# The feed forward's layer norm with its tokens on partitions

## The chip, the cores and the metric

The kernel runs on one core of a Trainium2 chip, in one launch. The metric is device time in microseconds (us); lower is better. The kernel before was timed in three runs: 2013.35 us is their median, 2007.73 the lowest and 2013.68 the highest. One execution was also profiled.

## What is computed

The input is one sequence of 2048 tokens with 128 channels. First comes an RWKV time mix with its own output norm (it takes the first 200 us and is not touched). Then come six layers, each an attention and a feed forward, both with a residual, and at the end a layer norm. Cut to what matters:

```python
def ffn_layer(x, g, bln, W1, b1, W2, b2):
    mu = x.mean(-1, keepdims=True)
    var = ((x - mu) ** 2).mean(-1, keepdims=True)
    xn = (x - mu) / jnp.sqrt(var + 1e-05) * g + bln
    hg = xn @ W1 + b1
    a, gate = jnp.split(hg, 2, -1)
    return a * jax.nn.gelu(gate, approximate=False) @ W2 + b2

for i in range(DEPTH):                      # DEPTH = 6
    x = attn_layer(shift_tokens(x), Wqkv[i], q_scale[i], k_scale[i], Wo[i]) + x
    x = ffn_layer(shift_tokens(x), ln_g[i], ln_b[i], W1[i], b1[i], W2[i], b2[i]) + x
```

`attn_layer` projects to 16 heads of 64, norms q and k to unit length, rotates them and attends inside windows of 32 tokens. `shift_tokens` takes half of the channels from the token before. All of it is float32.

## The kernel before, in words

The residual stream lies in two buffers, `xa` and `xb`, with the 128 channels on partitions and the tokens along the free axis. The 16 tiles of 128 tokens in 6 layers give 96 tile steps, and these are pipelined in software. Step `s` of `layers` (the functions `step` at L1011, L1048, L1145 and L1257, one for each engine) works on several tiles at once: it projects, norms and rotates q and k of tile `s+1` (live "p"), turns q and k of tile `s`, scores it and takes its softmax (live "a"), and does the mix with v, the output projection and the residual of tile `s-1` (live "b"). The feed forward goes by pairs of tiles, 256 tokens at a time, so that a part of it is in every second step:

- an **odd step** has "norm", the statistics of one pair's layer norm, and "down", the second matrix of an earlier pair;
- an **even step** has "up", which scales the pair whose statistics were taken in the odd step before, and multiplies it by the first matrix.

Each engine executes its own instructions strictly in the order written in its `step`, and waits on semaphores. Nothing else sets the order: there is no planner. A waiting instruction so holds up everything written behind it on its engine. Two places matter here. On PE, the order at the end of a step is v projection (L1352), down (L1359), the norm's matmul (L1364), the spread of the scale (L1371), the output projection `w_o` (L1377), the variance (L1383), `widen` (L1264), and then the next step's transposes of the probabilities (L1247). The latter wait for DVE's residual add `xb` (L1223), because `w_o`'s result lies in the bank that they write. On DVE the order is `unit` (L1176, twice), the first `centre_scores` (L1165, L1168), `norm_n` (L1214), the second `centre_scores`, `xa` (L1219), `xb` (L1223), `var_f` (L1228), `along` of k (L1234).

The layer norm is taken with the channels on partitions, so that its sums run across partitions, and PE does them:

1. POOL lays the shifted pair out in `shift_f` (L1025, L1026).
2. PE multiplies it by `centre`, which is the identity minus 1/128 everywhere: the result in `bank_b` is x minus its mean (L1364).
3. ACT copies that to `dev` (L1128) and squares it to `dev_sq` (L1130).
4. PE multiplies each tile of `dev_sq` by a column of 1/128: a variance for each token, tokens on partitions (L1383).
5. DVE adds the epsilon, from PSUM to `var_f` (L1228), and POOL raises it to the power -1/2, `rstd_f` (L1040).
6. In the even step ACT scales the rows of the identity by it, `rstd_diag` (L1098, twice), and PE multiplies that by ones: every partition now has every token's scale, in `bank_s` (L1371).
7. DVE multiplies `dev` by it, `norm_n` (L1214), ACT applies g and b of the norm, `normed` (L1121), and PE multiplies by the first matrix (`widen`, L1264).

POOL meanwhile does the rotation of q and k, all SBUF to SBUF on 128x1024 elements: `across` (L999) of q, `along` (L1032) of q, `rotated` (L1006) of q, `across` of k, [the power, in odd steps,] `rotated` of k. The `along` of k is DVE's (L1234). The first `across` of a step waits for DVE's `unit` of q.

The last norm, after the layers (`last_norm`, L1401), is written the other way: it turns the stream to tokens on partitions and uses DVE's batch-norm statistics (L1441, L1444) and a two-column `tensor_scalar` (L1450). It is not touched.

## Time and profile before

| what | value |
|---|---|
| median of 3 runs | 2013.35 us |
| span of the profiled execution, first to last instruction | 2010.7 us |
| PE busy (matmul) | 1805.9 us, 90% |
| DVE busy | 1557.0 us, 77% |
| POOL busy | 1455.2 us, 72% |
| ACT busy | 1164.3 us, 58% |
| mean granted TensorE clock | 0.969 of full |

The profile gives no time of its own for the profiled execution besides its span; the median of the runs is 2.65 us longer than that span. A busy share says how long an engine had an instruction in flight. It says neither that the engine was the limit nor that it ran at its best: the order of the queues and the last wait of each step say that.

### The profile page before, as it was taken

To read this page: it belongs to the slowest core of one execution; us is meant where nothing else is said; L and a number is where in the kernel's file an instruction comes from. 1 tells how busy PE (TensorE), PEld (TensorE's weight loads), DVE (VectorE), ACT (ScalarE), POOL (GpSimd) and SP (SyncE) were. 2 spreads that over 40 slices of the span, in tenths; PEclk is the share of its full clock that TensorE was granted. 3 is DMA by queue.
4 is the path that set the end of the run, shared out by engine and by line. 5 is a ranking of instruction groups with operands and counts; after the bars stand their busy time and mean duration, and the time that the engine had idled before them with its cause. 6 is when DMAs were issued, how large, how long until landed. Compare 5 with 4: busy or idle time off the path is not lost. (4 is left out here: it accounts for less than half of the span.)

```text
span 2010.7 us, 85596 instructions
## 1 busy us (share of the span) xinstructions
PE 1805.9 (90%) x34280; PEld 1311.9 (65%) x34280; DVE 1557.0 (77%) x2776; ACT 1164.3 (58%) x1966; POOL 1455.2 (72%) x967
## 2 busy tenths in 40 slices
PE   7774689999999999999999999999999999999995
PEld 3453466676776666766666666667676667676764
DVE  4764688887888878888788788887887888878864
ACT  2311356666666666666666666666666666666662
POOL 3221688877887778777877787778777877787771
PEclk9875899999999999999999999999999999999997
DMA  4000122223222223222223322233222232222220
GB/s 151 2 3 1 44 65 65 59 54 86 73 70 53 55 63 91 59 70 63 61 53 84 77 68 55 52 82 81 63 58 59 63 86 63 70 63 55 55 58 22
DMA packets 93581, 123.43 MB, mean 61 GB/s; under 512 B 27760, under 2 KB 41808, under 8 KB 93392
## 3 DMA queue, kind: packets, MB, share of 16 engines
q1 hardware_dynamic: 93232, 122.42, 24.2%
q8 instruction: 46, 0.75, 0.2%
q10 hardware_dynamic: 288, 0.13, 0.0%
q14 instruction: 15, 0.12, 0.0%
HBM read 20.74 MB, written 1.05 MB: 11 GB/s over the span
## 5 line engine op out<-in xcount | busy, mean ns | idle before, releaser
L999 POOL TENSOR_TENSOR across<-unit,turns 128x1024 f32<-128x1024 f32 x192 | 497.4, 2591 | 279.7 <-issue 268.4
L1006 POOL TENSOR_TENSOR rotated<-along,across 128x1024 f32<-128x1024 f32 x192 | 496.7, 2587 | 14.2
L1151 DVE TENSOR_REDUCE sums<-squares 128x16 f32<-128x1024 f32 x192 | 234.2, 1220 | 173.2 <-ACT squares L1054 173.1
L1247 PE MATMUL turn<-identity,rotated 128*128 128x128 f32 x1536 | 205.2, 277 | 36.4 <-POOL rotated L1006 36.4
L1247 PEld LDWEIGHTS turn<-identity,rotated 128*128 128x128 f32 x1536 | 172.6, 141 | 98.9 <-issue 83.4
L1032 POOL TENSOR_TENSOR along<-unit,turns 128x1024 f32<-128x1024 f32 x96 | 228.3, 2378 | 0.0
L1352 PE MATMUL proj_a<-w_qkv,shift_a 128*128 128x512 f32 x384 | 189.9, 617 | 36.4 <-DVE unit L1176 30.1
L1113 ACT COPY val<-proj_a 128x1024 f32<-128x1024 f32 x96 | 97.2, 1013 | 181.3 <-PE proj_a L1352 181.3
L1377 PEld LDWEIGHTS att<-o_t,w_o 128*128 128x128 f32 x1536 | 188.0, 193 | 6.1 <-issue 1.0
L1377 PE MATMUL att<-o_t,w_o 128*128 128x128 f32 x1536 | 188.3, 276 | 0.0
L1280 PE MATMUL proj_a<-w_qkv,shift_a 128*128 128x512 f32 x384 | 183.5, 601 | 4.3 <-POOL shift_a L988 3.0
L1089 ACT COPY k_t<-turn 128x512 f32<-128x512 f32 x192 | 103.4, 589 | 136.0 <-PE turn L1247 136.0
L1295 PE MATMUL proj_b<-w_qkv,shift_a 128*128 128x512 f32 x384 | 180.8, 593 | 0.0
L1234 DVE TENSOR_TENSOR along<-unit,turns 128x1024 f32<-128x1024 f32 x96 | 166.4, 1733 | 0.0
L1054 ACT ACTIVATE squares<-proj_a 128x1024 f32<-128x1024 f32 x96 | 98.3, 1024 | 114.2 <-PE proj_a L1280 114.2
L1340 PEld LDWEIGHTS turn<-k_t,q_t 64*32 64x32 f32 x12288 | 128.7, 105 | 41.9 <-issue 41.5
L1314 PE MATMUL att<-v_win,p_t 64*32 64x64 f32 x12288 | 154.6, 225 | 1.0 <-ACT p_t L1074 0.8
L1074 ACT COPY p_t<-att 128x512 f32<-128x512 f32 x192 | 103.2, 589 | 89.5 <-PE att L1247 89.5
L1314 PEld LDWEIGHTS att<-v_win,p_t 64*32 64x32 f32 x12288 | 136.3, 105 | 19.9 <-issue 17.3
L1157 DVE TENSOR_TENSOR heads_out<-att,inv_mass 128x512 f32<-128x512 f32 x192 | 123.7, 687 | 30.7 <-PE att L1314 30.7
L1340 PE MATMUL turn<-k_t,q_t 64*32 64x64 f32 x12288 | 144.6, 226 | 0.0
L1168 DVE TENSOR_TENSOR logits<-turn,row_max 128x512 f32<-128x512 f32 x192 | 132.8, 692 | 6.6
(203 smaller groups left out, 3445.2 us busy)
## 6 DMA issues: line engine op xcount, KB each, us to landing
v_win<-val SPq DMA_DIRECT2D x1536, 64.0 KB, 2.0
w_qkv<-wqkv_dram SPq DMA_DIRECT2D x18, 512.0 KB, 3.8
w_o<-wo_dram SPq DMA_DIRECT2D x6, 512.0 KB, 4.6
where<-positions_dram SPq DMA_DIRECT2D x1, 2048.0 KB, 11.4
w_ffn<-ffn_dram SPq DMA_DIRECT2D x12, 170.5 KB, 2.3
w_ffn<-ffn_dram SPq DMA_DIRECT2D x6, 192.0 KB, 2.3
x_tok<-x_dram SPq DMA_DIRECT2D x4, 256.0 KB, 4.3
out_dram<-final SPq DMA_DIRECT2D x4, 256.0 KB, 2.4
```

The costliest lines, as they stand in the source:

```text
L999: pool.tensor_tensor(a[:, :, ::-1, :], u, table, ALU.mult).then_inc(acrossed[j], 1)
L1006: pool.tensor_tensor(rotated[j][:, :, :], along[j][:, :, :], across[j][:, :, :], ALU.add).then_inc(rotated_in[j], 1)
L1032: pool.tensor_tensor(along[0][:, :, :], unit[0][:, :, :], turns[mine][:, 0, :].unsqueeze(1).broadcast_to([128, HEADS, HEAD]), ALU.mult).th ...
L1151: dve.tensor_reduce(sums[:, j, :], squares[j][:, :, :], AX.X, ALU.add).then_inc(summed[j], 1)
L1234: dve.tensor_tensor(along[1][:, :, :], unit[1][:, :, :], turns[mine][:, 2, :].unsqueeze(1).broadcast_to([128, HEADS, HEAD]), ALU.mult).the ...
L1247: mm = pe.transpose(bank[:, TILE * (i % 4):TILE * (i % 4) + TILE], buffer[:, TILE * i:TILE * i + TILE], identity[:, :])
L1280: mm = pe.matmul(bank_a[:, half, :], shift_a[mine][:, :], w_qkv[:, 512 * half:512 * half + 512], start=True, stop=True)
L1295: mm = pe.matmul(bank_b[:, half, :], shift_a[mine][:, :], w_qkv[:, base:base + 512], start=True, stop=True)
L1314: mm = pe.matmul(bank_s[WINDOW * w:WINDOW * w + WINDOW, par, HEAD * a_:HEAD * a_ + HEAD], p_t[rows, a_, WINDOW * w:WINDOW * w + WINDOW], v ...
L1340: mm = pe.matmul(bank_t[WINDOW * w:WINDOW * w + WINDOW, par, HEAD * a_:HEAD * a_ + HEAD], q_t[rows, a_, WINDOW * w:WINDOW * w + WINDOW], k ...
L1352: pe.matmul(bank_a[:, par, :].rearrange("p (a e) -> p a e", a=PAIRS), shift_a[mine][:, :], values[:, par, :, :], start=True, stop=True).th ...
L1377: mm = pe.matmul(bank_s[:, 0, 0:TILE], w_o[:, a_, :], o_t[:, a_, :], start=(a_ == 0), stop=(a_ == PAIRS - 1))
```

## The change

The norm is taken with tokens on partitions. The pair is transposed on PE instead of multiplied by `centre`, ACT copies it to SBUF (`f_tok`), and DVE takes batch-norm statistics of each tile there and adds the epsilon. In the even step DVE, not ACT and PE, applies mean and scale (`norm_tok`, two `tensor_scalar` ahead of the first `centre_scores`), PE turns the result back, and ACT applies g and b straight from PSUM. The matrices `centre` and `averager`, the square, the variance matmul, the scaled identity and its matmul by ones go. The core of the diff:

```diff
 @block.gpsimd
                     if live["norm"]:
                         pool.wait_ge(var_kept, h + 2)
-                        after(pool, rstd_laid, 2 * (h + 1))
+                        after(pool, scaled_f, 2 * (h + 1))
                         pool.tensor_tensor(rstd_f[:, :], var_f[:, :], minus_half[:, 0:2], ALU.pow).then_inc(rstd_made, 1)
 @block.scalar
-                    if live["up"]:
-                        act.wait_ge(rstd_made, h + 2)
-                        after(act, rstd_spread, h + 1)
-                        for j in range(2):
-                            act.activation(rstd_diag[:, j, :], identity[:, :], ACT.Copy, scale=rstd_f[:, j:j + 1])\
-                                .then_inc(rstd_laid, 1)
...
                     if live["up"]:
-                        act.wait_ge(scaled_f, h + 2)
+                        act.wait_ge(norm_turned, h + 2)
...
-                        act.activation(normed[:, :], norm_n[:, :], ACT.Identity, bias=w_ffn[:, F_B:F_B + 1],
+                        act.activation(normed[:, :], bank_s[:, 1, 0:TWO], ACT.Identity, bias=w_ffn[:, F_B:F_B + 1],
                                        scale=w_ffn[:, F_G:F_G + 1]).then_inc(normed_f, 1)
...
                     if live["norm"]:
-                        act.wait_ge(dev_made, h + 2)
-                        after(act, scaled_f, h + 1)
-                        act.copy(dev[:, :], bank_b[:, 0, 0:TWO]).then_inc(deviated, 1)
-                        after(act, var_made, h + 1)
-                        act.activation(dev_sq[:, :], bank_b[:, 0, 0:TWO], ACT.Square).then_inc(dev_squared, 1)
+                        act.wait_ge(f_turned, h + 2)
+                        after(act, scaled_f, 2 * (h + 1))
+                        act.copy(f_tok[:, :, :], bank_b[:, 0, 0:TWO].rearrange("p (j c) -> p j c", j=2)).then_inc(f_kept, 1)
 @block.vector
                         unite(0)
                         unite(1)
+                    if live["up"]:
+                        dve.wait_ge(rstd_made, h + 2)
+                        after(dve, norm_turned, h + 1)
+                        for j in range(2):
+                            dve.tensor_scalar(norm_tok[:, j, :], f_tok[:, j, :], f_moment[:, j, 0:1], rstd_f[:, j:j + 1],
+                                              ALU.subtract, ALU.mult).then_inc(scaled_f, 1)
                     if live["a"]:
                         centre_scores(0)
-                    if live["up"]:
-                        dve.wait_ge(rstd_spread, h + 2)
-                        after(dve, normed_f, h + 1)
-                        dve.tensor_tensor(norm_n[:, :], dev[:, :], bank_s[:, 1, 0:TWO], ALU.mult).then_inc(scaled_f, 1)
-                    if live["a"]:
                         centre_scores(1)
                     if live["down"]:
                         dve.wait_ge(narrowed, h + 1)
...
+                    if live["norm"]:
+                        dve.wait_ge(f_kept, h + 2)
+                        for j in range(2):
+                            dve.bn_stats(f_stat[:, j, :], f_tok[:, j, :]).then_inc(f_stated, 1)
+                        after(dve, scaled_f, 2 * (h + 1))
+                        dve.wait_ge(f_stated, 2 * (h + 2))
+                        stand_alone(dve, passed)
+                        for j in range(2):
+                            dve.bn_aggr(f_moment[:, j, :], f_stat[:, j, :]).then_inc(f_averaged, 1)
+                        dve.wait_ge(f_averaged, 2 * (h + 2))
+                        after(dve, rstd_made, h + 1)
+                        dve.tensor_scalar(var_f[:, :], f_moment[:, :, 1], LN_EPS, None, ALU.add).then_inc(var_kept, 1)
                     if live["b"]:
                         dve.wait_ge(attended, b + 1)
                         dve.tensor_tensor(xb[:, columns(b)], bank_s[:, 0, 0:TILE], xa[:, columns(b)], ALU.add)\
                             .then_inc(xb_ready, 1)
-                    if live["norm"]:
-                        dve.wait_ge(var_made, h + 2)
-                        after(dve, rstd_made, h + 1)
-                        dve.tensor_scalar(var_f[:, :], bank_b[:, 0, TWO:TWO + 2], LN_EPS, None, ALU.add)\
-                            .then_inc(var_kept, 1)
 @block.tensor
                     if live["norm"]:
                         pe.wait_ge(f_shifted, 2 * (h + 2))
-                        pe.matmul(bank_b[:, 0, 0:TWO], centre[:, :], shift_f[:, :], start=True, stop=True)\
-                            .then_inc(dev_made, 1)
+                        for j in range(2):
+                            mm = pe.transpose(bank_b[:, 0, TILE * j:TILE * j + TILE], shift_f[:, TILE * j:TILE * j + TILE],
+                                              identity[:, :])
+                        mm.then_inc(f_turned, 1)
                     if live["up"]:
-                        pe.wait_ge(rstd_laid, 2 * (h + 2))
+                        pe.wait_ge(scaled_f, 2 * (h + 2))
                         if live["b"]:
                             pe.wait_ge(o_laid, 2 * b + 2)
                             stand_alone(pe, passed)
-                        pe.matmul(bank_s[:, 1, 0:TWO], ones[:, :], diag_flat, start=True, stop=True).then_inc(rstd_spread, 1)
+                        for j in range(2):
+                            mm = pe.transpose(bank_s[:, 1, TILE * j:TILE * j + TILE], norm_tok[:, j, :], identity[:, :])
+                        mm.then_inc(norm_turned, 1)
...
-                    if live["norm"]:
-                        pe.wait_ge(dev_squared, h + 2)
-                        for j in range(2):
-                            mm = pe.matmul(bank_b[:, 0, TWO + j:TWO + j + 1], dev_sq[:, TILE * j:TILE * j + TILE],
-                                           averager[:, 0:1], start=True, stop=True)
-                        mm.then_inc(var_made, 1)
```

Where PE waited for `var_kept` before it reused `bank_b`, it now waits for `f_kept`. The setup loses POOL's fill of `averager` (L350) and DVE's `centre` (L1140).

## Rows read from the trace of the kernel before

**Rows 1.** Stretches, odd and even step: length, busy PE PEld DVE ACT POOL, PEclk, DMA.
```profile
998.10:1016.00 17.90, 16.75 (x332) 12.39 (x330) 12.89 (x27) 11.52 (x20) 13.93 (x11) 1.00 0.23 55
1016.00:1034.60 18.60, 17.67 (x332) 12.95 (x333) 16.77 (x27) 11.77 (x20) 15.37 (x10) 1.00 0.25 60
```
**Rows 2.** The timeline, PE: start us, us, the instruction, its count [idle before <- releaser].
```profile
1013.09 0.59 PE L1364 MATMUL proj_b<-shift_f,centre 128*128 128x256 f32 x2
1013.52 1.95 PE L1377 MATMUL att<-o_t,w_o 128*128 128x128 f32 x16
...
1016.09 1.06 PE L1247 MATMUL att<-identity,probs 128*128 128x128 f32 x8 [0.28 <-issue]
...
1027.84 1.96 PE L1352 MATMUL proj_a<-w_qkv,shift_a 128*128 128x512 f32 x4 [0.25 <-DVE unit L1176]
1030.07 1.95 PE L1377 MATMUL att<-o_t,w_o 128*128 128x128 f32 x16
1031.99 1.99 PE L1264 MATMUL proj_b<-normed,w_ffn 128*128 128x256 f32 x8
```
**Rows 3.** The timeline, DVE.
```profile
1015.69 0.29 DVE L1223 TENSOR_TENSOR xb<-att,xa 128x128 f32 x1 [1.63 <-PE att L1377]
...
1016.01 2.21 DVE L1234 TENSOR_TENSOR along<-unit,turns 128x1024 f32<-128x1024 f32 x1
...
1027.66 1.22 DVE L1176 TENSOR_TENSOR unit<-proj_b,inv_norm 128x1024 f32<-128x1024 f32 x1
...
1029.51 0.69 DVE L1168 TENSOR_TENSOR logits<-turn,row_max 128x512 f32<-128x512 f32 x1
```
**Rows 4.** The timeline, ACT.
```profile
1014.24 0.35 ACT L1128 COPY dev<-proj_b 128x256 f32<-128x256 f32 x1
...
1030.82 0.63 ACT L1061 ACTIVATE probs<-logits 128x512 f32<-128x512 f32 x1
1031.35 0.59 ACT L1121 ACTIVATE normed<-norm_n,w_ffn 128x256 f32<-128x256 f32 x1
```
**Rows 5.** The timeline, POOL.
```profile
1014.78 2.35 POOL L1006 TENSOR_TENSOR rotated<-along,across 128x1024 f32<-128x1024 f32 x1
1017.10 3.34 POOL L999 TENSOR_TENSOR across<-unit,turns 128x1024 f32<-128x1024 f32 x1
...
1030.19 2.37 POOL L1032 TENSOR_TENSOR along<-unit,turns 128x1024 f32<-128x1024 f32 x1
```
**Rows 6.** The timeline of the time mix, DVE and POOL.
```profile
96.41 1.75 DVE L622 TENSOR_TENSOR x_tok<-res_c,rstd 128x512 f32<-128x512 f32 x1 [1.14 <-POOL rstd L377]
97.56 1.72 POOL L383 TENSOR_TENSOR gate_b<-gate,half_rows 128x512 f32<-128x512 f32 x1
98.08 1.49 DVE L492 TENSOR_TENSOR rf<-rf,decay_one 128x256 f32<-128x256 f32 x1
```
**Rows 7.** Groups by line, DVE, before 215 us: xcount | busy us, mean ns | idle before.
```profile
L498 DVE TENSOR_TENSOR decay<-decay 128x128 f32<-128x128 f32 x4 | 1.1, 285 | 0.0
...
L474 DVE CAST band_bf<-band_f 128x128 bf16<-128x128 f32 x1 | 0.2, 218 | 0.0
```
**Rows 8.** The timeline of the last norm, DVE and POOL.
```profile
2001.29 0.36 DVE L1444 BATCH_NORM_AGGREGATE moment<-stat 128x2 f32<-128x6 f32 x4
...
2002.48 0.87 DVE L1441 BATCH_NORM_STATS2 stat<-total 128x6 f32<-128x128 f32 x4
...
2003.75 4.19 DVE L1450 TENSOR_SCALAR final<-total,moment,rstd_l 128x128 f32<-128x128 f32 x16
2003.92 1.03 POOL L1458 TENSOR_TENSOR rstd_l<-var_l,minus_half 128x4 f32<-128x4 f32 x1 [0.98 <-DVE var_l L1446]
```
**Rows 9.** Stretches with the same PE work at two clocks, columns as rows 1.
```profile
233.35:237.65 4.30, 4.30 (x13) 2.79 (x13) 1.36 (x2) 1.17 (x2) 4.17 (x3) 0.60 0.44 107
1016.09:1018.71 2.62, 2.62 (x12) 1.67 (x13) 2.62 (x2) 1.07 (x2) 2.62 (x2) 1.00 0.42 101
```
**Rows 10.** The timeline, PE, at the start of the slower of these two stretches.
```profile
233.35 1.91 PE L1247 MATMUL att<-identity,probs 128*128 128x128 f32 x8 [2.24 <-ACT probs L1061]
```

More of the change, by code:

```diff
@@ L198, in time_mix @@
                            "ident", "band", "level_masks"))
-    xa, xb, x_tok, identity, identity_bf, band_f, band_bf, averager, ones, minus_half = (
-        given[k] for k in ("xa", "xb", "x_tok", "identity", "identity_bf", "band_f", "band_bf", "averager",
+    xa, xb, x_tok, identity, identity_bf, band_f, band_bf, ones, minus_half = (
+        given[k] for k in ("xa", "xb", "x_tok", "identity", "identity_bf", "band_f", "band_bf",
                            "ones", "minus_half"))
@@ L354, in _ @@
                     pool.memset(state[:, :], 0.0).then_inc(cleared, 1)
[L355 removed]
+                pool.wait_ge(constants_made, 2)
                 pool.wait_ge(x_laid, 4)
@@ L824, in layers @@
         given[k] for k in ("load_projection", "load_wo", "load_up", "load_down"))
-    xa, xb, identity, identity_bf, band_bf, averager, ones, minus_half = (
-        given[k] for k in ("xa", "xb", "identity", "identity_bf", "band_bf", "averager", "ones", "minus_half"))
+    xa, xb, identity, identity_bf, band_bf, ones, minus_half = (
+        given[k] for k in ("xa", "xb", "identity", "identity_bf", "band_bf", "ones", "minus_half"))
     bank_a, bank_b, bank_s, bank_t = (given[k] for k in ("proj_a", "proj_b", "att", "turn"))
@@ L863, in layers @@
         shift_f = sb("shift_f", [128, TWO])
-        dev = sb("dev", [128, TWO])
-        dev_sq = sb("dev_sq", [128, TWO])
+        f_tok = sb("f_tok", [128, 2, TILE])
+        f_stat = sb("f_stat", [128, 2, 6])
+        f_moment = sb("f_moment", [128, 2, 2])
         var_f = sb("var_f", [128, 2])
         rstd_f = sb("rstd_f", [128, 2])
-        rstd_diag = sb("rstd_diag", [128, 2, TILE])
-        norm_n = sb("norm_n", [128, TWO])
+        norm_tok = sb("norm_tok", [128, 2, TILE])
         normed = sb("normed", [128, TWO])
@@ L875, in layers @@
         warmed = sem("warmed")
-        cleared, centre_made = sem("cleared"), sem("centre_made")
+        cleared, magic_made = sem("cleared"), sem("magic_made")
         shifted = sem("shifted")
@@ L893, in layers @@
         o_turned, o_laid, attended, xb_ready = sem("o_turned"), sem("o_laid"), sem("attended"), sem("xb_ready")
-        f_shifted, dev_made, deviated, dev_squared = (
-            sem(k) for k in ("f_shifted", "dev_made", "deviated", "dev_squared"))
-        var_made, var_kept, rstd_made, rstd_laid, rstd_spread, scaled_f, normed_f = (
-            sem(k) for k in ("var_made", "var_kept", "rstd_made", "rstd_laid", "rstd_spread", "scaled_f", "normed_f"))
+        f_shifted, f_turned, f_kept, f_stated, f_averaged = (
+            sem(k) for k in ("f_shifted", "f_turned", "f_kept", "f_stated", "f_averaged"))
+        var_kept, rstd_made, scaled_f, norm_turned, normed_f = (
+            sem(k) for k in ("var_kept", "rstd_made", "scaled_f", "norm_turned", "normed_f"))
         widened, gelued, gated, narrowed, xa_ready = (
@@ L1021, in step @@
                         pool.wait_ge(xb_ready, s - 1)
-                        after(pool, dev_made, h + 1)
+                        after(pool, f_turned, h + 1)
                         after(pool, rotated_in[1], p if live["p"] else STEPS)
@@ L1253, in _ @@
                 heads_flat = heads_out[:, :, :, :].rearrange("p a b e -> p (a b e)")
-                diag_flat = rstd_diag[:, :, :].rearrange("p a t -> p (a t)")
                 values = w_qkv[:, 2 * INNER:].rearrange("i (a b e) -> i b a e", a=PAIRS, b=2)
```

14 lines of the change are left out of this document (4 added, 10 removed).

## The prediction, made before the changed kernel ran

> **What bounds the kernel now.** I read four views: the stretches, then the timelines of PE, DVE and ACT, then POOL's. An odd and an even step take 36.5 us together at the full clock, with PE busy in 34.4 of them [rows 1]: PE is the bound, nearly without gaps, and what delays PE at a step's end is paid in full. The timelines say where a step can be delayed. In an odd step `w_o` ends at 1015.47, DVE's `xb` follows, and the next transposes start 0.1 us after `xb` ends [rows 2, 3]; here DVE is on the path. In an even step `widen` starts at 1031.99, when `w_o` ends (1032.02) and just after ACT's `normed` ends (1031.94) [rows 2, 4]: two chains arrive together. The v projection waits for DVE's `unit` of q [rows 2], so what lies between the mix and it is covered.
>
> POOL is no bound, but it touches DVE. Its four large operations follow each other from the end of `unit` of q [rows 5]. The `along` of DVE at 1016.01 took 2.21 us, against 1.22 for an operation of this size elsewhere [rows 3]: it ended 1.09 us after POOL's `rotated` did (1017.13), and POOL's `across` behind it took 3.34, not 2.35 [rows 5]. In the time mix the same happens three times running: `x_tok` (1.75 where 128x512 takes 0.69 [rows 3]) ends at 98.16, POOL's `gate_b` beside it takes 1.72, and DVE's next, issued at 98.08, ends only at 99.57, after `gate_b` (99.28) [rows 6]. So a DVE operation that shares a resource with POOL waits until POOL's current instruction ends, POOL's next one waits for it, and **DVE's second waits for that one in turn**. All these read two SBUF tensors. The variance add and `norm_n` of before read PSUM and at most one SBUF tensor.
>
> **Does this reach the new operations?** The two `norm_tok` and the new `var_f` are `tensor_scalar` from SBUF to SBUF, with one tensor input. No row has one beside a large POOL operation. Against a wait: only one input. For it: a cast of 128x128 takes 218 ns, where a two-input operation of the same size takes 285 [rows 7]; the 67 ns that are saved on 128 elements say that a one-input operation fetches faster than one element at a time, so by a second path, and the one at hand is the one that second inputs use. The final norm's `tensor_scalar` ran 16 times in 4.19 us beside a POOL power, unhindered [rows 8]; but that power reads four numbers a partition and computes for a microsecond, and says little. I take it that they wait. The Trainium skill, "SBUF — State Buffer", section "Who interferes with whom", says so: `tensor_scalar` between SBUF operands can run in a mode that takes both of DVE's port pairs, one of which is POOL's, and whoever is second is fully blocked; by that rule every added `tensor_scalar` waits as below, without it none does, and no run shows it yet.
>
> **The even step, step by step.** Removed from PE: the spread, 0.43 us by the like matmul's distance to its successor (1013.09 to 1013.52) [rows 2]; added: two transposes, 0.13 each (1.06 for 8) [rows 2]. Removed from ACT: two `rstd_diag`, beside PE work. Removed from DVE: `norm_n`. Added to DVE: two `norm_tok` at 0.26 us of queue each (4.19 us for 16) [rows 8].
> - With no wait (lower bound): 0.52 us ahead of the first `centre_scores`; `logits` ends at 1030.7 and not 1030.20 [rows 3], before ACT is free for `probs` at 1030.82 [rows 4]. `normed` starts when it did. From PSUM it may be some 0.05 shorter. The step gains 0.05 us, not the 0.2 that PE saves.
> - With waits (upper bound, which I take): `unit` of k ends at 1028.88 [rows 3] in the middle of POOL's `across`. The first `norm_tok` waits until 1030.2, where `along` starts [rows 5], and ends at 1030.5. `along` (2.37) then runs first, to 1032.8, and the second ends at 1033.1. Queued behind it are both `centre_scores`; waiting for it is PE, with the transposes, `w_o` and `widen` behind them. On DVE row maximum and `logits` (0.7 each) end at 1034.5, then ACT's `probs` 0.63 and `normed` 0.59 [rows 4]: `widen` starts at 1035.7. On PE `w_o` would end at 1035.3. So **+3.7 us**.
>
> In that case PE stands idle from 1029.8 to 1033.1. After an idle stretch of 2.24 us [rows 10] the same transposes and q projection took 4.30 us at a granted clock of 0.60 (a mix of 1.2 and 2.4 GHz) and not 2.62 at 1.00 [rows 9]: 1.7 us more. Here `w_o` would end at 1037.0 and take over from the ACT chain: +1.3 more, **+5.0 in all** (between 3.7 and 6.5, if `widen` starts slow too).
>
> **The odd step.** Removed from PE: the centring (0.43) and the variance matmuls, which ran while PE would have waited for `xb` anyway: nothing for those; added two transposes (0.26). `w_o` ends 0.2 earlier, at 1015.3. Removed from ACT: `dev_sq`. On DVE, ahead of `xb`: ACT's copy ends at 1014.6 as before [rows 4]; two statistics 0.48, two aggregates 0.22 [rows 8], `var_f` 0.2 with the gaps.
> - No wait: `xb` starts at 1015.6, 0.1 earlier than at 1015.69. Gain 0.1 us.
> - With a wait: `var_f` is issued at about 1015.4 in the middle of `rotated`, which ends at 1017.13 [rows 5]. Then `xb`, 0.29, with PE's transposes behind it, at 1017.65 where it was 1016.09: **+1.55 us**. PE idles 2.3 us, as in rows 10; I charge half of the 1.7 us, because the clock may or may not fall: +0.85, **2.4 in all** (1.5 to 3.3). DVE's `along` now queues behind `across`, to 1020.6; the sums of squares are 0.5 late, which the mix covers. POOL's power comes later too, and is wanted only a step on.
>
> The Trainium skill, "Vector Engine (DVE) Microarchitecture Reference", section "Performance modes", says that one source in SBUF with two elements per partition still takes the two-port mode, which is `var_f`'s shape; by it the odd step pays, and without it only the even step does. No DMA is changed or moved.
>
> **The sum.** 46 even steps have "up" with POOL at work, and 46 odd ones "norm". (5.0 + 2.4) x 46 = 340 us, less some 2 us in the last four steps, where the chain is shorter and POOL idle. The profiled span is 2010.7, and 2.65 below the median: 2013.35 + 338 is about **2350 us**.
>
> **The rivals.**
> - *Only the large ones wait*: `var_f` reads two numbers and slips through. 4.9 x 46 = 225, about 2238 us. For it: its size. It is told by `xb` starting at about 0.1 after `w_o` in odd steps.
> - *Both `norm_tok` go through in one wait*, against rows 6: done at 1030.8, `widen` at 1033.5, +1.5, and PE's idle 1.0 us costs no clock. (1.5 + 2.4) x 46 = 180: about 2193 us.
> - *The other side, no wait at all*: one-input operations do not meet POOL. It decides in the first `norm_tok`: under 0.4 us beside `across`, the waits are nil. Then 0.15 x 46 = 7 and 2 in the tail: about 2004 us, 0.45% faster. For it: the final norm, unhindered beside a power [rows 8], and that no row shows the contrary. Its error of 0.1 us a step is worth 5 us, so it is partly "the same".
>
> **How the numbers follow.** A measurement can tell about 0.3%, 6 us, from no change. Both wait: 0.50; only the large: 0.18; one wait: 0.10; none: 0.20; anything else 0.02. The range leaves the last two out: from the one-wait case less 40 us for its clock share, 2150, to both-wait with (5.9 + 3.1) x 46, 2425. The own range of the likeliest is 2255 to 2425. Faster 0.12, same 0.07, slower 0.81.
>
> **What would show it.** Right: `norm_tok` with a mean well over 0.34 us (about 1.6 and 2.6 for the pair), `var_f` about 1.7, idle PE before its transposes ended by DVE `norm_tok`, a second idle before the transposes of the probabilities ended by `xb`, POOL's operations at times longer than 2.35, and a granted clock below 1.00 in the loop. Wrong: `norm_tok` at 0.34 each, with PE as busy as before. A mean in between with a clock of 1.00 would say that the waits are real and my charge for the clock is not.

## The result, and the profile after

Four executions of the changed kernel took 2262.7 to 2280.8 us, median **2275.2 us**. The kernel before had a median of 2013.3 us beside it. The ratio is **1.131 (95%: 1.128 to 1.134)**, so the change makes the kernel 13% slower, and the forecast (2350, range 2150 to 2425) was right in sign and 75 us too high. The profiled execution has a span of 2260.5 us, 14.7 below the median of the changed kernel's runs, and a mean granted clock of 0.934 (before 0.969). It is the fastest of the four (2262.7 us); the other three have a clock of 0.919 to 0.922.

First the page's line of busy times of the kernel after. DVE gains 315.8 us of busy time, PE only 39, and POOL has lost some:

```profile
PE 1845.2 (82%) x34088; PEld 1321.9 (58%) x34088; DVE 1872.8 (83%) x3015; ACT 1131.0 (50%) x1822; POOL 1410.9 (62%) x966
```

DVE got no such amount of new work, so its instructions must be long for another reason. The groups by line of the kernel after, 400 to 2100 us, say which. A row has line, engine, operation, out<-in, shapes, count | busy us, mean ns of one | idle before it:

```profile
L996 POOL TENSOR_TENSOR across<-unit,turns 128x1024 f32<-128x1024 f32 x162 | 381.6, 2356 | 449.1 <-issue 449.1
...
L1230 DVE TENSOR_TENSOR along<-unit,turns 128x1024 f32<-128x1024 f32 x81 | 212.3, 2621 | 0.0
...
L1201 DVE TENSOR_SCALAR norm_tok<-f_tok,f_moment,rstd_f 128x128 f32<-128x128 f32 x80 | 152.8, 1949 | 0.0
...
L1037 POOL TENSOR_TENSOR rstd_f<-var_f,minus_half 128x2 f32<-128x2 f32 x41 | 69.5, 1694 | 0.0
...
L1221 DVE TENSOR_SCALAR var_f<-f_moment 128x2 f32<-128x2 f32 x41 | 66.0, 1611 | 1.4
```

Two of these rows have a counterpart in the kernel before (400 to 1800 us):

```profile
L1040 POOL TENSOR_TENSOR rstd_f<-var_f,minus_half 128x2 f32<-128x2 f32 x39 | 27.5, 705 | 0.0
...
L1228 DVE TENSOR_SCALAR var_f<-proj_b 128x2 f32<-128x2 f32 x38 | 5.7, 150 | 0.0
```

`norm_tok` takes 1.95 us on average (1.52 the first of a pair, 2.38 the second) where the same form took 0.26 in the last norm [rows 8]. `var_f` takes 1.61 us for two numbers a partition; read from PSUM, it took 0.15 in the kernel before. POOL's power, also of two numbers, went from 0.71 to 1.69. All three are far above what their size explains.

The timeline of the kernel after at the end of an odd step (start us, us, instruction [idle before <- releaser]) answers to the odd step of [rows 2, 3, 5]:

```profile
1198.30 2.34 POOL L1003 TENSOR_TENSOR rotated<-along,across 128x1024 f32<-128x1024 f32 x1
...
1198.77 0.25 DVE L1218 BATCH_NORM_AGGREGATE f_moment<-f_stat 128x2 f32<-128x6 f32 x2
1199.05 1.61 DVE L1221 TENSOR_SCALAR var_f<-f_moment 128x2 f32<-128x2 f32 x1
...
1200.58 0.28 DVE L1224 TENSOR_TENSOR xb<-att,xa 128x128 f32 x1
...
1200.60 2.36 POOL L996 TENSOR_TENSOR across<-unit,turns 128x1024 f32<-128x1024 f32 x1
1200.78 3.26 DVE L1230 TENSOR_TENSOR along<-unit,turns 128x1024 f32<-128x1024 f32 x1
...
1200.96 1.06 PE L1242 MATMUL att<-identity,probs 128*128 128x128 f32 x8 [2.19 <-issue]
```

`var_f` is in flight from 1199.05 to 1200.66, and POOL's `rotated` ends at 1200.64. The aggregates just ahead of it, which started in the middle of the same `rotated`, took 0.25 for two. `xb` stands behind `var_f`, and PE's transposes behind `xb`. Then DVE's `along` comes after POOL's `across` and not before it as in [rows 3, 5]: it takes 3.26, and `across` no longer takes 3.34. The two have changed places. By the pages, `across` is busy for 452.3 us in all where it was 497.4, and that is where POOL's busy time went; what `rotated` lost besides (42.1 us), the longer power takes up.

The even step of the kernel after, as a timeline, answers to the even step of [rows 2 to 5]:

```profile
1212.40 1.96 PE L1346 MATMUL proj_a<-w_qkv,shift_a 128*128 128x512 f32 x4 [0.27 <-DVE unit L1164]
1212.44 2.34 POOL L996 TENSOR_TENSOR across<-unit,turns 128x1024 f32<-128x1024 f32 x1 [3.87 <-issue]
...
1213.35 3.82 DVE L1201 TENSOR_SCALAR norm_tok<-f_tok,f_moment,rstd_f 128x128 f32<-128x128 f32 x2
...
1214.75 2.33 POOL L1029 TENSOR_TENSOR along<-unit,turns 128x1024 f32<-128x1024 f32 x1
...
1217.32 0.66 PE L1368 MATMUL att<-identity,norm_tok 128*128 128x128 f32 x2 [2.96 <-DVE norm_tok L1201]
...
1217.77 3.28 PE L1375 MATMUL att<-o_t,w_o 128*128 128x128 f32 x16
...
1219.07 0.55 ACT L1112 ACTIVATE normed<-att,w_ffn 128x256 f32<-128x256 f32 x1
...
1220.88 1.89 PE L1258 MATMUL proj_b<-normed,w_ffn 128*128 128x256 f32 x8
```

The pair of `norm_tok` is in flight until 1217.17, 0.09 after POOL's `along` ends (1217.08): the first waited for `across`, the second for `along`. PE stood idle for 2.96 us. In this step `w_o` then took 3.28 us where it had 1.95 [rows 2]. The stretches of the kernel after show the granted clock behind it (columns as in [rows 1]):

```profile
1217.30:1221.30 4.00, 3.98 (x20) 3.96 (x21) 2.47 (x5) 2.47 (x4) 4.00 (x2) 0.59 0.00 0
1195.00:1217.70 22.70, 16.94 (x330) 12.00 (x329) 21.47 (x32) 10.19 (x16) 18.32 (x12) 0.99 0.19 46
```

But the clock doesn't fall in every such step. Another even step of the same execution, PE alone, has the same idle time and keeps its speed:

```profile
1046.10 1.95 PE L1346 MATMUL proj_a<-w_qkv,shift_a 128*128 128x512 f32 x4 [0.27 <-DVE unit L1164]
1051.01 0.41 PE L1368 MATMUL att<-identity,norm_tok 128*128 128x128 f32 x2 [2.96 <-DVE norm_tok L1201]
1051.30 2.02 PE L1375 MATMUL att<-o_t,w_o 128*128 128x128 f32 x16
1053.35 1.99 PE L1258 MATMUL proj_b<-normed,w_ffn 128*128 128x256 f32 x8
```

Two rows of the waits of the kernel after (who <- whom: us in all, times, longest) give the totals from 400 to 2100 us:

```profile
PE att L1368 <- DVE norm_tok L1201: 118.4, 40, 3.0
...
PE att L1242 <- issue: 89.7, 41, 2.2
```

They are 208 us in 41 pairs of steps, 5.1 a pair. For every kernel below, step lengths are distances between the starts of successive transposes of the probabilities on PE, averaged from 300 to 1880 us:

| kernel | even step | odd step | granted clock, 400 to 1800 us |
|---|---|---|---|
| before | 18.60 | 17.88 | 1.00 |
| after | 22.82 (21.38 to 25.52) | 19.22 | 0.96 |

Below, the clock "fell" where the granted clock went from 2.4 to 1.2 GHz for a stretch. Of the 36 pairs of steps of the kernel after (an even step and the odd one behind it) between 300 and 1880 us, 16 have no such stretch. They average 41.05 us, and all 36 average 42.0.

### The profile page after: what moved, and what is told of

Same layout as the page of the kernel before. It is cut to its first block and busy times, and to the rows that moved or that the text cites. A ratio compares the mean times of both kernels' runs of the same rounds, so it can differ in the third digit from the quotient of the medians.

```text
span 2260.5 us, 85394 instructions
## 1 busy us (share of the span) xinstructions
PE 1845.2 (82%) x34088; PEld 1321.9 (58%) x34088; DVE 1872.8 (83%) x3015; ACT 1131.0 (50%) x1822; POOL 1410.9 (62%) x966
## 5 line engine op out<-in xcount | busy, mean ns | idle before, releaser
L996 POOL TENSOR_TENSOR across<-unit,turns 128x1024 f32<-128x1024 f32 x192 | 452.3, 2356 | 524.8 <-issue 513.6
L1003 POOL TENSOR_TENSOR rotated<-along,across 128x1024 f32<-128x1024 f32 x192 | 454.6, 2368 | 62.8 <-DVE along L1230 54.7
L1230 DVE TENSOR_TENSOR along<-unit,turns 128x1024 f32<-128x1024 f32 x96 | 248.2, 2585 | 0.0
L1375 PE MATMUL att<-o_t,w_o 128*128 128x128 f32 x1536 | 228.8, 313 | 0.0
L1375 PEld LDWEIGHTS att<-o_t,w_o 128*128 128x128 f32 x1536 | 219.5, 228 | 3.3 <-issue 1.0
L1346 PE MATMUL proj_a<-w_qkv,shift_a 128*128 128x512 f32 x384 | 189.5, 616 | 30.2 <-DVE unit L1164 24.2
L1274 PE MATMUL proj_a<-w_qkv,shift_a 128*128 128x512 f32 x384 | 198.8, 644 | 3.2 <-POOL shift_a L986 1.9
L1058 ACT ACTIVATE probs<-logits 128x512 f32<-128x512 f32 x192 | 121.1, 632 | 157.4 <-DVE logits L1156 153.3
L1242 PE MATMUL att<-identity,probs 128*128 128x128 f32 x768 | 108.4, 288 | 107.0 <-issue 98.5
L1201 DVE TENSOR_SCALAR norm_tok<-f_tok,f_moment,rstd_f 128x128 f32<-128x128 f32 x96 | 176.9, 1882 | 0.9 <-POOL rstd_f L1037 0.9
L1242 PEld LDWEIGHTS att<-identity,probs 128*128 128x128 f32 x768 | 91.9, 148 | 122.0 <-issue 115.7
```

What stands on the lines that cost most here:

```text
L996: pool.tensor_tensor(a[:, :, ::-1, :], u, table, ALU.mult).then_inc(acrossed[j], 1)
L1003: pool.tensor_tensor(rotated[j][:, :, :], along[j][:, :, :], across[j][:, :, :], ALU.add).then_inc(rotated_in[j], 1)
L1201: dve.tensor_scalar(norm_tok[:, j, :], f_tok[:, j, :], f_moment[:, j, 0:1], rstd_f[:, j:j + 1], ALU.subtract, ALU.mult).then_inc(scaled_f, 1)
L1230: dve.tensor_tensor(along[1][:, :, :], unit[1][:, :, :], turns[mine][:, 2, :].unsqueeze(1).broadcast_to([128, HEADS, HEAD]), ALU.mult).the ...
L1242: mm = pe.transpose(bank[:, TILE * (i % 4):TILE * (i % 4) + TILE], buffer[:, TILE * i:TILE * i + TILE], identity[:, :])
L1274: mm = pe.matmul(bank_a[:, half, :], shift_a[mine][:, :], w_qkv[:, 512 * half:512 * half + 512], start=True, stop=True)
```

## The experiments

The theory: a DVE `tensor_scalar` from SBUF to SBUF doesn't run beside a large POOL operation, it waits for POOL's current one, and two in a row wait for two. The rivals: only large ones wait; the layout itself (transposes, statistics, more DVE work) costs the time; and, for the part of it that is the clock, that there is hardly such a part. Ratios below are to the kernel before, run on the same chip.

**1. Take each operation off DVE, then both.** `eps_pool` has POOL add the epsilon. `norm_act` lets ACT apply mean and scale (`Identity` with scale and bias), for which POOL makes the offset behind its `rotated`. `both_off` has both edits.

```diff
 eps_pool, @block.gpsimd
+                        pool.wait_ge(f_averaged, 2 * (h + 2))
+                        after(pool, scaled_f, 2 * (h + 1))
+                        pool.tensor_tensor(var_f[:, :], f_moment[:, :, 1], eps_f[:, :], ALU.add).then_inc(var_kept, 1)
                         pool.wait_ge(var_kept, h + 2)
-                        after(pool, scaled_f, 2 * (h + 1))
 norm_act, @block.gpsimd, behind add_turned(1, p)
+                        pool.tensor_tensor(scaled_m[:, :], f_moment[:, :, 0], rstd_f[:, :], ALU.mult).then_inc(mean_scaled, 1)
...
+                        pool.tensor_tensor(offset_f[:, :], scaled_m[:, :], minus_one[:, :], ALU.mult).then_inc(offset_made, 1)
 norm_act, @block.scalar, ahead of o_t
+                            act.activation(norm_tok[:, j, :], f_tok[:, j, :], ACT.Identity, bias=offset_f[:, j:j + 1],
+                                           scale=rstd_f[:, j:j + 1]).then_inc(scaled_f, 1)
```

Expected of `eps_pool`: 

> From the changed kernel the epsilon's add goes from DVE to POOL, ahead of the power; nothing else. Port theory (a DVE tensor_scalar from SBUF to SBUF waits until POOL's running instruction ends, and var_f's 1.61 us are such a wait): xb follows the output projection at once, the idle of 2.2 us before the transposes of the probabilities shrinks to about 0.6, the odd step goes from 19.2 to about 17.8 us, the even one stays at 22.8: 46 x 1.4 = 64 us less, about 2211 us. Rival (the time is that of the longer DVE queue, not of a wait): the instruction is worth its 0.15 us, 46 x 0.15 = 7 us, about 2268 us.

Expected of `norm_act`: 

> From the changed kernel the two norm_tok go from DVE to ACT (scale and offset, the offset made by two small POOL operations at the end of the odd step), at the place where ACT scaled the identity before; var_f stays on DVE. Port theory: ACT waits for nothing of POOL's, so the even step goes back from 22.8 to about 18.6 to 18.8 us and the odd one stays at 19.2: about 2275 - 46 x 4.1 = 2086 us, with the granted clock back at 1.00 in the loop. Rival (the even step is long because the transposes and w_o stand behind a chain through two engines, wherever the scaling is done, and DVE's queue is longer): the even step keeps most of its length, only the 0.5 us of DVE queue go, about 2250 us.

Expected of `both_off`: 

> Both of the above: the batch-norm statistics and the transposes stay, but DVE has no tensor_scalar from SBUF to SBUF left in the loop. Port theory: all of the loss is gone; what is left is my estimate of the change without waits, 0.05 us gained in the even step and 0.1 in the odd one: 2003 to 2015 us, at or just under the kernel before. Rival (a good part of the loss is the layout change itself): clearly over the kernel before, 2050 us or more.

| kernel | median us | ratio (95%) | even step | odd step | clock |
|---|---|---|---|---|---|
| `eps_pool` | 2189.2 | 1.087 (1.085 to 1.090) | 23.00 | 17.52 | 0.96 |
| `norm_act` | 2062.2 | 1.025 (1.023 to 1.027) | 18.34 | 19.27 | 1.00 |
| `both_off` | 2028.1 | 1.008 (1.006 to 1.010) | 19.20 | 17.73 | 1.00 |

Each edit mends its own step and not the other. `eps_pool` came out 22 us and `norm_act` 24 us below what was expected of them, both far from their rivals (2268 and 2250). What is left in `norm_act` shows in its groups by line, 400 to 1800 us: `norm_tok` takes 0.50 on ACT, and `var_f` takes what it did:

```profile
L1233 DVE TENSOR_SCALAR var_f<-f_moment 128x2 f32<-128x2 f32 x37 | 59.6, 1610 | 1.3
...
L1107 ACT ACTIVATE norm_tok<-f_tok,offset_f,rstd_f 128x128 f32<-128x128 f32 x76 | 33.6, 497 | 0.0
```

And in the waits of `norm_act`, same stretch, PE stands idle for 2.2 us in each odd step, while the granted clock of the loop is 1.00:

```profile
PE att L1254 <- issue: 81.1, 37, 2.2
```

So 2.2 us of idle PE in each odd step cost next to no clock here: it fell behind one of them, at 848 us, where the q projection then took 3.22 us and not 1.88, and the even step 19.88 and not 18.30. Experiment 2 shows that this isn't safe. `eps_pool` adds one more thing. POOL's power takes 0.71 again, and not 1.69. With `var_f` gone from DVE's queue, DVE's `along` no longer comes late beside it, which fits a power that waits for `along`; no run tested that alone. `both_off` missed its expectation by 13 to 25 us: the waits are gone and 0.6 us is left in the even step. Experiment 4 is about that.

**2. One instruction in place of the pair.** `one_scale` applies the first tile's mean and scale to both tiles in one instruction of 128x256; it so leaves out the second tile's own mean and scale.

```diff
-                        for j in range(2):
-                            dve.tensor_scalar(norm_tok[:, j, :], f_tok[:, j, :], f_moment[:, j, 0:1], rstd_f[:, j:j + 1],
-                                              ALU.subtract, ALU.mult).then_inc(scaled_f, 1)
+                        dve.tensor_scalar(norm_tok[:, :, :], f_tok[:, :, :], f_moment[:, 0, 0:1], rstd_f[:, 0:1],
+                                          ALU.subtract, ALU.mult).then_inc(scaled_f, 2)
```

> From the changed kernel the two norm_tok become one tensor_scalar over both tiles, with the first tile's mean and scale for both (this leaves out the second tile's own). The number of waits is then one and not two. Port theory with strict alternation: it waits for the rest of the first across only and takes about 1.8 us against 3.8 for the pair; PE's idle before the transposes falls from 3.0 to about 1.0 us and costs no clock; the even step goes from 22.8 to about 19.7: 46 x 3.1 = 140 us less, about 2135 us. If the two went through in one wait already, the edit is worth one instruction, 0.3 us a step, about 2262 us.

Measured: 2171.5 us, ratio 1.080 (1.078 to 1.082), even step 20.39, odd step 19.71. The instructions of its line (count: min/median/max ns, first and last start):

```profile
L1200 DVE TENSOR_SCALAR norm_tok<-f_tok,f_moment,rstd_f x39: 1584/1589/1592, 336.3 to 1860.6; 128x256 f32<-128x256 f32 x39
```

The same elements in one instruction take 1.59 us, in two 3.82. The number of instructions sets the wait, not the work: each is let in only after one more of POOL's.

The direction was as stated, but 2135 was 36 us too low: the clock was expected to cost nothing, and it is 0.97 from 400 to 1800 us. PE's idle time before the transposes of `norm_tok` is down to 0.7 us, and the odd step's is 2.2 as in `norm_act`; yet here the clock fell behind the latter in 29 of 39 cases, as in this one:

```profile
1004.22 1.72 PE L1241 MATMUL att<-identity,probs 128*128 128x128 f32 x8 [2.20 <-issue]
1005.73 2.95 PE L1273 MATMUL proj_a<-w_qkv,shift_a 128*128 128x512 f32 x4
```

From 1004.2 to 1008.5 us the granted clock is 0.60. Even steps with such a fall take 20.78 us, the other ten 19.23. Without a fall the even step is so 0.6 us longer than before, and a fall adds 1.55. The length of PE's longest idle time is the same in `norm_act` and `one_scale`, and doesn't decide whether the clock falls.

**3. The wait by itself, in the kernel before.** `before_two` puts a `tensor_scalar` of 128x2 on constants ahead of the odd step's `xb`; `before_reduce` has a reduction with the same operands in that place. Nothing uses either result.

```diff
 before_two
+                            dve.tensor_scalar(spare[:, :], ones[:, 0:2], LN_EPS, None, ALU.add).then_inc(spared, 1)
 before_reduce
+                            dve.tensor_reduce(spare[:, :], ones[:, 0:2].unsqueeze(2), AX.X, ALU.add).then_inc(spared, 1)
```

Expected of `before_two`: 

> The kernel before, with one tensor_scalar more on DVE in the odd step: two numbers a partition, SBUF to SBUF, result unused, behind the wait for the output projection and ahead of xb. It is issued in the middle of POOL's rotated. Port theory: it takes about 1.5 us and not 0.17, the odd step grows from 17.9 to about 19.3, the even one stays: 46 x 1.4 = 64 us more, about 2076 us. Rival (such a short operation is its own price): 46 x 0.2 = 9 us, about 2021 us.

Expected of `before_reduce`: 

> The same place, the same two numbers from the same SBUF tensor to the same one, but as a tensor_reduce over an axis of length one. If the wait belongs to the form (an operation that takes POOL's ports), this one has none, as the statistics had none in the changed kernel: it takes about 0.15 us, 46 x 0.2 = 9 us more, about 2020 us. If every DVE operation from SBUF to SBUF waits for POOL, it is as slow as the tensor_scalar, about 2076 us.

Measured: `before_two` 2061.7 us, ratio 1.025 (1.023 to 1.028), odd step 19.25, even step 18.35. `before_reduce` 2009.1 us, ratio 1.000 (0.999 to 1.001). The instructions of the spare tile, first in `before_two`:

```profile
L1227 DVE TENSOR_SCALAR spare<-ones x42: 1642/1652/1665, 326.0 to 1867.7; 128x2 f32<-128x2 f32 x42
```

and in `before_reduce`:

```profile
L1227 DVE TENSOR_REDUCE spare<-ones x44: 154/155/157, 320.6 to 1890.0; 128x2 f32<-128x2 f32 x44
```

Same place, same two numbers, same memory, another operation: a tenth of the time. This is without any transposed norm, so the layout has no part in it. The rival "only the large ones wait" falls here as well. The even step got 0.25 us shorter behind the delayed odd one, as it did in `norm_act`: a late step is partly made up for in the next. That is 12 of the 14 us by which `before_two` stayed below the expected 2076. `before_reduce` cost nothing, where 9 us were expected.

**4. The 0.6 us left over.** My first theory was that in `both_off` the small POOL operations stand ahead of the `rotated` of k and make it late. `both_off_late` puts all of them behind it; `before_late` does the same with the power of the kernel before, in case there was something to gain there.

```diff
 both_off_late and before_late
                         cross(1, p, mine)
+                        add_turned(1, p)
                     if live["norm"]:
...
-                    if live["p"]:
-                        add_turned(1, p)
```

Expected of `both_off_late`: 

> The kernel without either tensor_scalar (2028 us), with POOL's rotated of k moved ahead of the norm's four small operations. Theory: what is left of the loss there is POOL's, because the epsilon, the power and what is around them (0.9 us) stand ahead of rotated, for which PE then waits 1.0 us in every even step (0.6 before). With rotated first that idle goes and the even step falls from 19.2 to about 18.3 us: 46 x 0.9 = 41 us less, about 1987 us, under the kernel before. Rival (the 0.6 us of the even step are ACT's, whose two norm_tok take 1.0 us where the two scalings of the identity took 0.7, ahead of the copies of o_t): no gain, 2028 us.

Expected of `before_late`: 

> The kernel before with the same move alone: POOL's rotated of k ahead of the power. It shows what of the gain of the run before is the move's and not the new norm's. PE's idle of 0.59 us before the transposes of k goes, but the v projection behind it waits for DVE's unit with 0.25 us to spare, so at most 0.35 us in each even step, 46 x 0.35 = 16 us: 1997 us; if unit is the true bound, nothing, 2013 us.

Measured: `both_off_late` 2026.3 us, ratio 1.009 (1.007 to 1.011), where 1987 was expected; `before_late` 2010.8 us, ratio 1.001 (0.999 to 1.002), no gain. That theory has fallen. The timeline of `both_off_late` in an even step suggests another:

```profile
1028.29 0.79 POOL L1025 TENSOR_TENSOR turns<-where,scales 128x256 f32 x1
...
1028.52 0.61 DVE L94 TENSOR_TENSOR root_work<-root_work,sums_min 128x32 f32<-128x32 f32 x1
...
1029.38 0.32 DVE L98 SCALAR_TENSOR_TENSOR inv_norm<-root_work,inv_norm 128x32 f32<-128x32 f32 x1
...
1031.86 0.67 PE L1360 MATMUL proj_a<-w_qkv,shift_a 128*128 128x512 f32 x1 [0.94 <-DVE unit L1187]
```

With four small POOL operations a pair, three more than before, POOL's `turns` and its copies come to where DVE's chain of small root operations runs (0.19 each when alone). The first of the two DVE operations shown ends at 1029.13, just after `turns` does (1029.08). So DVE's chain seems to wait for POOL, `unit` comes late, and PE's v projection waits 0.94 us for it; in [rows 2] it was 0.25. Experiment 5 takes the added POOL operations away.

**5. No SBUF `tensor_scalar` on DVE, and nothing more on POOL.** If both readings hold, a version without either must keep the layout and lose nothing. `psum_moments` has DVE write the aggregates to PSUM and add the epsilon and turn the mean's sign from there, behind `xb`; ACT makes the offset and applies the norm.

```diff
 @block.vector
-                            dve.bn_aggr(f_moment[:, j, :], f_stat[:, j, :]).then_inc(f_averaged, 1)
...
-                        dve.tensor_scalar(var_f[:, :], f_moment[:, :, 1], LN_EPS, None, ALU.add).then_inc(var_kept, 1)
+                            dve.bn_aggr(bank_b[:, 0, TWO + 2 * j:TWO + 2 * j + 2], f_stat[:, j, :]).then_inc(f_averaged, 1)
...
+                        moments = bank_b[:, 0, TWO:TWO + 4].rearrange("p (j m) -> p j m", m=2)
+                        dve.tensor_scalar(var_f[:, :], moments[:, :, 1], LN_EPS, None, ALU.add).then_inc(var_kept, 1)
+                        dve.tensor_scalar(minus_mean[:, :], moments[:, :, 0], -1.0, None, ALU.mult).then_inc(mean_kept, 1)
 @block.scalar
+                            act.activation(offset_f[:, j:j + 1], minus_mean[:, j:j + 1], ACT.Copy,
+                                           scale=rstd_f[:, j:j + 1]).then_inc(offset_made, 1)
...
+                            act.activation(norm_tok[:, j, :], f_tok[:, j, :], ACT.Identity, bias=offset_f[:, j:j + 1],
+                                           scale=rstd_f[:, j:j + 1]).then_inc(scaled_f, 1)
```

> The new norm with no use of POOL's ports and no added POOL work: the aggregates go to PSUM, DVE adds the epsilon and negates the mean from there behind xb, ACT makes the offset (two tiny operations) and scales the tokens. Theory: the 0.6 us that the kernel without either tensor_scalar still lost in the even step came from its three added POOL operations, which pushed POOL's table product and copies into DVE's chain of nine root operations (two SBUF inputs each; 0.61 and 0.32 instead of 0.19 for three of them). Without them the even step falls from 19.2 to 18.3 to 18.6 us, the odd one stays at 17.7: 1985 to 2005 us, at or just under the kernel before. Rival (those 0.6 us are ACT's longer work ahead of the o_t copies, which is longer still here): 2028 us or more.

Measured: **2001.2 us, ratio 0.9952 (0.9937 to 0.9966)**, faster than both kernels, with steps of 18.61 and 17.74 us and a clock of 1.00. The timeline of its odd step, to set beside that of the kernel after:

```profile
1042.10 2.35 POOL L1005 TENSOR_TENSOR rotated<-along,across 128x1024 f32<-128x1024 f32 x1
1042.57 0.26 DVE L1226 BATCH_NORM_AGGREGATE proj_b<-f_stat 128x2 f32<-128x6 f32 x2
1042.82 0.29 DVE L1229 TENSOR_TENSOR xb<-att,xa 128x128 f32 x1
1043.03 0.15 DVE L1234 TENSOR_SCALAR var_f<-proj_b 128x2 f32<-128x2 f32 x1
...
1043.21 0.95 PE L1252 MATMUL att<-identity,probs 128*128 128x128 f32 x7 [0.65 <-issue]
```

The same `var_f`, read from PSUM in the middle of the same `rotated`, takes 0.15 and not 1.61. The even step is back at its old length, and the time lies in the expected range (1985 to 2005). That speaks for the added POOL operations as the cause of the 0.6 us of experiment 4, and against ACT's longer work, the rival there: ACT has two operations more here than in `both_off`. The steps save 0.13 us a pair, 6 us in 46 pairs; the rest of the 10 us lies outside the steps compared and was not followed up.

**6. The clock's share.** `wo_first` has PE do `w_o` before it waits for `norm_tok`. `ballast` fills PE's wait with 20 transposes of the identity into an unused part of a bank, so that PE isn't idle while DVE is as late as before.

```diff
 wo_first
+                    if live["b"]:
+                        pe.wait_ge(wo_in, (layer_of(b) + 1) * 16)
...
+                        mm.then_inc(attended, 1)
                     if live["up"]:
                         pe.wait_ge(scaled_f, 2 * (h + 2))
...
                         mm.then_inc(norm_turned, 1)
-                    if live["b"]:
-                        pe.wait_ge(wo_in, (layer_of(b) + 1) * 16)
...
-                        mm.then_inc(attended, 1)
 ballast, ahead of the transposes of norm_tok
+                    if live["up"] and live["b"]:
+                        pe.wait_ge(o_laid, 2 * b + 2)
+                        for j in range(20):
+                            pe.transpose(bank_s[:, 1, TWO:TWO + TILE], identity[:, :], identity[:, :])
```

Expected of `wo_first`: 

> The changed kernel with PE's output projection ahead of the two transposes of norm_tok, and so no longer behind the wait for DVE. Port theory: norm_tok is as late as before (3.8 us for the pair), so the wait stays, but the projection fills 2 of its 3 us, xb comes earlier, and widen is bound by the chain norm_tok, transposes, probs, normed alone: it starts about 1.2 us earlier where the clock had fallen, and 0.1 where not. The even step goes from 22.8 to about 21.6: 46 x 1.2 = 55 us less, 2220 us. If the projection behind the wait were the cost by itself, the even step would be back near 19.6, 2125 us.

Expected of `ballast`: 

> The changed kernel with 20 transposes of the identity (2.4 us of PE work, result unused) while PE waits for norm_tok. It measures the clock's part by itself. Theory: the even steps that take 22.5 to 25.5 us are those with the granted clock at half after the idle of 3.0 us; with PE busy the clock stays at 1.00 and all even steps come to the shortest one's 21.4: 46 x 1.4 = 64 us less, 2211 us. If the clock isn't what makes them longer, there is no gain or a small loss, 2275 us or more.

Measured: `wo_first` 2292.0 us, ratio 1.139 (1.138 to 1.141), steps 23.86 and 18.91, clock 0.94. `ballast` 2239.3 us, ratio 1.113 (1.112 to 1.115), steps 21.64 and 19.69, clock 1.00. PE in an even step of `ballast`:

```profile
1007.50 2.35 PE L1365 MATMUL att<-identity 128*128 128x128 f32 x20
1010.66 0.41 PE L1372 MATMUL att<-identity,norm_tok 128*128 128x128 f32 x2 [0.82 <-DVE norm_tok L1201]
```

The 20 transposes end 0.82 us before `norm_tok` does, so they cost next to nothing themselves (even steps in which the clock didn't fall: 21.47 us, in the kernel after 21.43). `ballast` saves 1.131 less 1.113, 35 us by the medians (some 7 either way by the two intervals) and 23 us by the spans of the two profiled executions, or 0.5 to 0.8 us a pair.

This is a lower bound for the clock's share, since the clock still fell behind the odd step's wait in 4 of the 37 even steps (23.05 us). The kernel after gives the share itself, by its pairs of steps without a fall: 42.0 less 41.05, 0.95 us a pair, 44 us in 46. The waits, and whatever else the new layout changes, then have 41.05 less 36.48, 4.57 us a pair, 210 us. The 52 us that are left of the 262 hold those 44, the longer times of the other three executions with their lower clock, and what lies outside the steps compared.

`ballast` was expected at 2211, with 1.4 us saved in each even step. But part of what a fall at the wait for `norm_tok` costs is given back: the odd step behind it takes 18.9 us, and behind an even step without a fall 19.6.

`wo_first` was expected at 2220 and went the other way. PE in one of its even steps says why:

```profile
1030.21 1.95 PE L1367 MATMUL att<-o_t,w_o 128*128 128x128 f32 x16
1033.36 0.41 PE L1376 MATMUL att<-identity,norm_tok 128*128 128x128 f32 x2 [1.20 <-DVE norm_tok L1201]
1035.71 1.99 PE L1258 MATMUL proj_b<-normed,w_ffn 128*128 128x256 f32 x8 [1.94 <-ACT normed L1112]
```

In the kernel after, `widen` starts 2.34 us after the transposes (1051.01 to 1053.35), and here 2.35: in both it is ACT's chain to `normed` that takes this long, and in the kernel after `w_o` merely fills it. Moved ahead, it saves nothing and leaves two idle times of 3.14 us together. In the profiled execution the clock fell in all 36 pairs of steps, against 20 of 36 in the kernel after. That explains the longer steps of this execution. It doesn't settle the 17 us between the medians, because the mean clock of all runs of `wo_first` (0.924 to 0.926) is no lower than in three of the four runs of the kernel after.

## Why the prediction was right in sign, and 75 us too high

- **What bounds the kernel, and where a step can be delayed**: held. Both waits of DVE came out on PE whole, at the two places named: the transposes of the norm, and those of the probabilities behind `xb`.
- **"I take it that they wait"**: held, for the large and the small, and strictly in turn, as read from [rows 6]. `norm_tok` has a mean of 1.95 us, `var_f` 1.61; the pair was expected at 1.6 and 2.6 and has 1.52 and 2.38. It is shown by each operation taken away (experiment 1), by one in place of two (2), by the operation alone in the kernel before (3) and by its PSUM form (5). The Trainium skill, "SBUF — State Buffer", section "Who interferes with whom", gave this rule, and the trace agrees: `var_f` takes 1.61 us beside `rotated` and 0.15 when it reads PSUM. The Trainium skill, "Vector Engine (DVE) Microarchitecture Reference", section "Performance modes", has two elements a partition in the two-port mode too, and the 1.65 us of `before_two` agree.
- **The even step's wait, +3.7**: too high by 0.6. From the v projection's start to `widen` is 7.25 us in the step at 1046.10, where before it was 4.15 [rows 2]: +3.1. Of the difference 0.35 is in the first half: the second `norm_tok` ended 0.09 after POOL's `along`, where I had charged 0.24 for a late `along` and 0.3 for the instruction's own time. The rest is in ACT's chain behind it, 2.34 for 2.6. Another 0.3 is given back earlier in the same step, which is shorter when the odd step before it was late (18.35 in `before_two`, 18.34 in `norm_act`). Such a step is 21.4 us long, +2.8.
- **The odd step's wait, +1.55**: near. PE's idle time is 2.19 us (forecast 2.3), the step is 19.22 on average, +1.34, and `before_two`, with nothing but this wait, has +1.37. Where the even step before kept its clock the odd one is 19.6, +1.7, since DVE's late `along` makes `hidden` late, for which PE's k projection waits 0.6 us.
- **The clock, 1.3 + 0.85 a pair**: the term that was mis-sized most. I took one pair of stretches [rows 9] from the thin beginning of the layers, and charged its 1.7 us for every wait of the even step (1.3 after the overlap with ACT's chain) and for half of those of the odd one. The price of one fall was near: 1.55 us in `one_scale`. How often the clock falls was wrong. Ahead of [rows 9] it had been at 0.50 from 224.4 to 228.3 us, and from there to the end of the idle time PE was busy in 6.03 of 8.95 us, where the loop has 34.4 of 36.5. In the full loop it fell behind the odd step's wait in 1 of 41 cases (`norm_act`), 29 of 39 (`one_scale`) and 11 of 36 (the kernel after). At the even step's 2.96 us it fell in 19 of 36, and what that costs is partly given back in the next step. The clock's share is 0.95 us a pair, not 2.15. That is 55 of the 340 us forecast.
- **The sum**: forecast 5.25 of waits and 2.15 of clock a pair; measured 4.57 and 0.95 in the profiled execution, which is 12.5 us shorter than the median one. Both terms are too high, and the clock makes most of it. The upper end of the range rests on 5.9 and 3.1 us a pair, for which the prediction shows no working.
- **The rivals**: "only the large ones wait" gave 2238, and `ballast` lies at 2239 with every wait in place: the same number from another mechanism, which a time alone couldn't have told apart; `var_f` at 1.61 does. "One wait" was priced at +1.5 an even step with no clock lost. `one_scale` has +1.8, but only 0.6 of it is there when the clock doesn't fall, so this price was near by luck. "No wait" is refuted for this kernel; its gain of 0.15 us a pair is near what `psum_moments`, which has no such wait, came to (0.13).
- **What would show it**: all named signs came but one. POOL's operations are not longer than before but shorter (`across` 2.36 on average, before 2.60), since its `across` no longer comes second to DVE's `along`; DVE's `along` is longer in its place (2.62 for 1.71).

## What to carry to other kernels

Before a DVE operation is added, look at what it reads and writes and what POOL runs at that moment: a `tensor_scalar` between SBUF operands costs the rest of POOL's current instruction (here always a `tensor_tensor` between SBUF operands), however small it is, and a second one behind it costs a whole further one. Read it from PSUM, use a reduction or a statistics operation, or give it to ACT, but count what is then added to POOL too. One slow stretch gives the price of one fall of the clock. How often it falls must come from a loop as dense as the one it is charged to, and two kernels with the same idle time of 2.2 us differed in it by 1 of 41 and 29 of 39.

## What was not expected

- POOL seems to pay as well: its power of two numbers took 1.69 us instead of 0.71 where DVE's `along` came late. Nothing waited for it.
- The batch-norm statistics and aggregates, SBUF to SBUF, ran unhindered beside POOL's `along` and `rotated` (0.48 and 0.25 us for two), as did a reduction (0.155).
- The same idle time of 2.96 us on PE, at the same place of the loop and in one execution, was followed by a granted clock of 0.59 in one step and by an unslowed `w_o` (2.02) in another. What decides between them stays open, as it does between `norm_act` and `one_scale`; the lengths of the even steps (21.38 to 25.52) show that both are common.
- ACT's `normed` takes 0.55 us from PSUM and took 0.59 from SBUF [rows 4].
